# Two output tiles at a time, in alternating banks, in the hidden layers of a post-norm transformer block

## The reference

```
x = L0_attn_x                                  # 8 x 512 x 256, fp32
x = layernorm(x + attention(x))                # 16 heads of 16, its own causal weighting
x = layernorm(x + ffn(x))

def ffn(x):                                    # weights are ternary times 8, scales per output
    h = silu((x @ w1.T) * s1) * ((x @ w2.T) * s2)      # 256 -> 1024
    h = gelu((h @ h1.T) * sh1)                          # 1024 -> 1024
    h = gelu((h @ h2.T) * sh2)                          # 1024 -> 1024
    return (h @ w3.T) * s3                              # 1024 -> 256
```

## Time and profile before

| | |
|---|---|
| median of 3 runs | 1271.8 us (1270.05 to 1274.11) |
| the profiled execution: its own time | 1269.87 us |
| its span, first to last instruction | 1267.8 us |
| granted TensorE clock, mean | 0.989 |
| PE busy | 1184.9 us, 93% |
| PE weight loads busy | 804.8 us, 63% |
| DVE, ACT, POOL busy | 751.9, 653.6, 211.2 us |

### The profile page before, as it was taken

One profiled execution on the slowest core, in us unless ns is written; L12 is line 12 of the kernel. 1 busy time (PEld: TensorE's weight loads), 2 busy tenths in 40 slices (PEclk: granted clock), 3 DMA queues, 4 the chain that ended last, 5 costly groups with the idle time before them and its releaser, 6 DMA issues.

```text
span 1267.8 us, 24071 instructions
## 1 busy us (share of the span) xinstructions
PE 1184.9 (93%) x8222; PEld 804.8 (63%) x8222; DVE 751.9 (59%) x1266; ACT 653.6 (52%) x960; POOL 211.2 (17%) x238
## 2 busy tenths in 40 slices
PE   5899998999989899878999999999999999999997
PEld 2444444444444344435788888888888888888886
DVE  3568889788888888675544434435335254453444
ACT  4688888888888888756314224233232242322411
POOL 2434333334333343220000000000000000000000
PEclk8999999999999999989999999999999999999999
DMA  4555657676574756339200100000000001000000
GB/s 150 116 137 135 199 146 216 157 199 181 168 205 132 232 141 171 86 92 365 87 34 1 34 18 0 33 17 17 33 0 33 17 3 47 0 33 17 0 33 18
DMA packets 62543, 117.27 MB, mean 93 GB/s; under 512 B 8992, under 2 KB 14624, under 8 KB 62496
## 3 DMA queue, kind: packets, MB, share of 16 engines
q1 hardware_dynamic: 62064, 116.12, 32.3%
q10 hardware_dynamic: 432, 0.52, 0.2%
HBM read 46.35 MB, written 19.92 MB: 52 GB/s over the span
## 4 chain that ended last, share of the span: by engine, by line
PE 78%; ACT 7%; DVE 7%; issue 6%; DMA 1%; POOL 0%; DVEq 0%; ACTq 0%; POOLq 0%; SPq 0%
PE score_banks L1251 51%; PE acc_bank L1163 7%; PE score_banks L1135 6%; PE misc_bank L1090 2%; PE misc_bank L1231 2%; DVE w_ring L816 2%; PE misc_bank L1127 2%; ACT e_ring L613 2%; ACT w_ring L620 2%; PE misc_bank L1098 2%; PE misc_bank L1210 1%; ACT acc_copy L649 1%; PE misc_bank L1100 1%; PE misc_bank L1099 1%; ACT q_full L575 1%
## 5 line engine op out<-in xcount | busy, mean ns | idle before, releaser
L689 ACT ACTIVATE f_h_full<-score_banks,f_scales 128x512 f32<-128x512 f32 x128 | 87.5, 689 | 340.6 <-PE score_banks L1251 340.5
L816 DVE TENSOR_TENSOR w_ring<-score_banks,keep 128x1024 int32<-128x1024 int32 (+1 forms) x192 | 194.1, 1040 | 27.3 <-PE score_banks L1135 26.8
L1251 PE MATMUL score_banks<-f_ha_hi,f_w_all 128*128 128x512 f32 x512 | 204.0, 399 | 0.0
L1251 PE MATMUL score_banks<-f_hb_hi,f_w_all 128*128 128x512 f32 x512 | 203.6, 398 | 0.0
L1251 PE MATMUL score_banks<-f_hb_lo,f_w_all 128*128 128x512 f32 x512 | 201.4, 393 | 0.0
L1251 PE MATMUL score_banks<-f_ha_lo,f_w_all 128*128 128x512 f32 x512 | 200.8, 392 | 0.0
L620 ACT ACTIVATE w_ring<-w_ring 128x1024 f32<-128x1024 f32 (+1 forms) x192 | 176.7, 922 | 17.4 <-DVE w_ring L816 16.8
L613 ACT ACTIVATE e_ring<-score_banks 128x1024 f32<-128x1024 f32 (+1 forms) x192 | 158.1, 877 | 33.0 <-PE score_banks L1135 33.0
L491 POOL TENSOR_SCALAR_AFFINE_SELECT e_ring<-e_ring 128x512 f32<-128x512 f32 (+1 forms) x96 | 79.1, 824 | 309.8 <-DVE e_ring L801 169.4
L1001 DVE CAST f_ha_hi<-f_h_full 128x512 fp32r<-128x512 f32 x64 | 27.3, 427 | 160.0 <-ACT f_h_full L689 159.8
L1251 PEld LDWEIGHTS score_banks<-f_ha_hi,f_w_all 128*128 128x128 f32 x512 | 96.1, 188 | 24.6
(11 more groups left out here) (144 smaller groups left out, 1795.2 us busy)
## 6 DMA issues: line engine op xcount, KB each, us to landing
piece<-in_wf SPq DMA_DIRECT2D x44, 256.0 KB, 2.9
wf_copy<-piece SPq DMA_DIRECT2D x44, 256.0 KB, 3.0
ky_stack<-ky_hi SPq DMA_DIRECT2D x64, 128.0 KB, 2.4
ky_stack<-ky_lo SPq DMA_DIRECT2D x64, 128.0 KB, 2.4
k_stack<-k_hi SPq DMA_DIRECT2D x64, 128.0 KB, 2.7
k_stack<-k_lo SPq DMA_DIRECT2D x64, 128.0 KB, 2.6
f_w_all<-wf_copy SPq DMA_DIRECT2D x2, 4096.0 KB, 26.0
f_x_turn<-x SPq DMA_DIRECT2D x9, 512.0 KB, 3.3
```

Of the source, the lines that this page charges most:

```text
L689: nc.scalar.activation(h_full[m % 2][:], f_bank[m % F_RING], ACT.Gelu, scale=scales[:, 1 + layer, m:m + 1]).then_inc(gelu_done, 1)
L816: nc.vector.tensor_tensor(w_ring[:, t % RING, 2 * i:2 * i + 2, 0:cols].bitcast(I32), pair_banks(w_pair(t, i), cols).bitcast(I32), keep[:, ...
L1251: mm = nc.tensor.matmul(out, left.bitcast(dt), right.bitcast(dt), start=first and n == 0, stop=last and n == 1)
```

## The change

The nested function `rows` and its split into early and late contraction tiles go. The hidden layers now run over pairs of output tiles (0, 1), (2, 3), (4, 5), (6, 7). In a pair, for each contraction tile, the order is `hi` with tile m's weights into its bank, `hi` with tile m+1's weights into the other bank, `lo` with m's weights, `lo` with m+1's. The number of matmuls and weight loads is as before. Both waits for free banks stand ahead of a pair, both `f_ready` signals come with its last two matmuls, and what `attention_tail` does behind two tiles now all stands behind the pair. The transposes of the next input stay behind 64 matmuls of h2.

```
-                    def rows(m, kts):
-                        n = FT * layer + m
-                        if 0 in kts:
+                    for m in range(0, FT, 2):
+                        two = (m, m + 1)
+                        for tile in two:
+                            n = FT * layer + tile
                             if n < F_RING:
                                 pe.wait_ge(gate_done, FT * c + FT - 1 + n // 2)
                             else:
                                 pe.wait_ge(gelu_done, 2 * FT * c + n - F_RING + 1)
-                        for kt in kts:
+                        for kt in range(FT):
                             if m == 0:
                                 pe.wait_ge(h_split, 3 * FT * c + FT * layer + kt + 1)
-                            mm = both(dt, f_bank[m % F_RING], f_w[name][:, kt, P * m:P * m + P],
-                                      hi[:, kt, :], lo[:, kt, :], kt == 0, kt == FT - 1)
-                        if FT - 1 in kts:
-                            mm.then_inc(f_ready, 1)
-
-                    rows(0, range(FT - LATE))
-                    rows(1, range(FT - LATE))
-                    for m in range(FT):
-                        rows(m, range(FT - LATE if m < 2 else 0, FT))
+                            for part, half in enumerate((hi, lo)):
+                                for tile in two:
+                                    mm = nc.tensor.matmul(f_bank[tile % F_RING], f_w[name][:, kt, P * tile:P * tile + P].bitcast(dt),
+                                                          half[:, kt, :].bitcast(dt), start=kt == 0 and part == 0,
+                                                          stop=kt == FT - 1 and part == 1)
+                                    if kt == FT - 1 and part == 1:
+                                        mm.then_inc(f_ready, 1)
                         if first:
-                            attention_tail(layer, m)
-                        if layer == 1 and m == 3:
+                            for tile in two:
+                                attention_tail(layer, tile)
+                        if layer == 1 and m == 2:
```

## The result

| | before | after |
|---|---|---|
| median of 20 runs each | 1272.22 us (1269.16 to 1275.44) | 1275.97 us (1273.21 to 1277.68) |
| ratio, 95% interval | | 1.0026 [1.0016, 1.0035] |
| span of the profiled execution | 1267.8 us | 1273.4 us |

The change makes the kernel 0.26% slower, some 3.3 us by the ratio (the two medians lie 3.75 us apart); 1274.5 was forecast on a median before of 1271.8, which is +2.7 us. The page of the changed kernel, to be laid beside the earlier trace rows: span, TensorE, and its granted clock in 40 slices.

What follows compares the result with a forecast made beforehand. PE was taken to bound the kernel, busy 93% of the span. Stream 0, w3 cover 0.3 and chunk 0 2.4 sum to +2.7 us, on a median of 1271.8 giving 1274.5 us; range 1264 to 1283 us.

Steps and rivals of the forecast that it cites:

- What bounds it: Whole kernel: PE, busy 93% of the span; in chunks 1 to 7 the chain is PE alone, without waits.
- The stream at 2048 x 0: Hidden layers' 2048 matmuls: changing bank and weights each time leaves the start-to-start gap unchanged, 0 us; bounds -12 to +10 us.
- Cover ahead of w3: Before w3 in each chunk: DVE finishes tile 7 at 3.22 us, needed at 3.23; 0.04 us a chunk, 0.3 in all.
- Flip: Chunk 0: tile 0 ends 1 matmul before the flip instead of 4, so PE waits longer for ACT's copy, +0.7 us.
- Transposes: Chunk 0, behind tiles 4 and 5: the second transpose now waits for ACT's copy of the first, +0.84 us.
- Projections: Chunk 0, behind tiles 6 and 7: the second projection now waits for DVE's reading of the first, +0.9 us.
- one resumption less: Chunk 0, behind tiles 4 and 6: gives back some 0.1 us each, left in the rounding.
- Sum: Whole kernel: 0 + 0.3 + 2.4 = +2.7 us, a median of 1274.5 us; chance 0.56.
- Rival 1: Hidden layers: alternation speeds up the stream, to 1266.3 us (chance 0.10) or 1262.5 us (chance 0.10).
- Rival 2: Every hidden matmul: the slower 238 ns gap becomes the rule, +10 + 2.7, 1284.5 us; chance 0.15.
- Rival 3: Ahead of w3: DVE becomes the bound, two tiles 0.6 us late in each chunk, 1279 us; chance 0.09.
- Rival 4: Chunk 0: stalls lie beside something, so nothing measurable changes; inside the forecast's own range, 1271 to 1278; no separate chance.

## Why the prediction was right

- **What bounds it**: confirmed. The loop chunks are PE alone and did not change in length.
- **The stream at 2048 x 0**: confirmed to 0.1 us in 30: h1's 128 matmuls span 29.63 us before and after, h2's 30.44 and 30.46. The argument from the single bank change at a tile's start held when it became the rule. That it would could not be read from one such place; the profile after shows it for 2048 matmuls.
- **Cover ahead of w3, 3.22 against 3.23 us, 0.3 us in all**: the narrowness was real (a load 0.03 us late), its cost was not; 0 in place of 0.3.
- **Flip +0.7**: 0.69 by the rows above.
- **Transposes +0.84**: 0.89. The second starts 635.42 - 634.31 = 1.11 us behind the first instead of 0.44, a wait of 0.67: ACT's copy starts 0.03 us after the transpose and not 0.18. The restart adds 0.22, as below.
- **Projections +0.9**: 1.1. The wait itself is 0.84 us (645.25 to 646.09), near the 0.89 computed. What the term left out is in the chain's last rows: the second projection takes 1.99 us, not 1.73, as PE starts anew behind the wait, with the clock granted in full. The same on the transpose, 0.66 instead of 0.44. I had written of one resumption less and counted none more, though the earlier trace rows had the price: the flip, behind a wait, takes 0.63 us there, and a transpose of four matmuls of the same shape, behind none, 0.44.
- **Sum**: +2.7 forecast; chunk 0 gave +2.8, loop 0, timed +3.3 [2.0, 4.5]. The closeness of the two is in part luck. No term had the two restarts (0.22 + 0.26 us). Against them stand waits that were 0.2 us shorter than computed in all (0.67 for 0.84, 0.84 for 0.89) and the 0.3 us of w3 that did not come.
- **Rival 1** rested on new weights having the shorter gap. The profile after refutes it: all gaps have new weights, half are still 238 ns. My remark against it, that the pattern comes from how the stream is entered, was half the truth. It holds for 238/229 against the seven-beat pattern of h2 behind its transposes, but the level of 233 instead of 227 has another cause, the distance of operands. **Rival 2** fell likewise. **Rival 3** needed 0.2 us of delay a chunk and got 0.03. **Rival 4**, no measurable change: 20 runs of each tell the change from zero, but +3.3 us is less than the 3.8 us that the prediction itself took as the least that can be told from no change. The forecast lay in that band too, so what came true is its small size and its place.

## What to carry to other kernels

When a stream of matmuls has no wait left, read the distance between starts, layer against layer. A constant difference between streams of the same shape can be worth more than a reordering of them: here reordering gave 0 in the loop and 128 bytes of placement 1.2%. And when independent pieces that share one buffer are moved behind a common point, count each reader that used to be covered, and a restart for each new wait (0.2 to 0.3 us each here). And before two single executions are compared, compare their granted clocks.

## What the hardware showed that I had not expected

The distance in memory between the weights and the moving operand sets the gap of the 512-column matmuls of this kernel. A multiple of 256 bytes between their tiles gives 226.7 ns; 128 or 192 more than one (before, and with 64 bytes) gives 232 to 233.3. Absolute placement did not matter in the one move tried: both moved by 128 bytes changed nothing. These are the only offsets tried; 64 was not, and nothing here shows the mechanism. The rule is not carried over to other shapes: the 256-column matmuls of w3, whose stationary operand is the hidden tile and whose moving operand is the weights, took 119.9 ns at the distance of before and with 128 or 384 bytes more, and 117.8 ns with 64, where the 512-column ones were slow.

The irregular part of the gaps depends on the entry to the stream: one wait or eight transposes in front can turn the 238/229 alternation of h1 into a pattern of seven gaps (228 to 241 ns) with the lower mean of 232.4 ns, at the same distance of operands. It need not: behind the flip's wait in chunk 0, before has the seven gaps and after the alternation. At a multiple of 256 bytes the gaps of h1 and h2 in a loop chunk are 226 to 228 ns, but for the first few behind the transposes (224 to 236 ns with 128 bytes).
